# Edge sort of a ViT tower: column totals in the tower's prologue, other cuts and costs for the ranks, all row ranks beside the first experts

## The reference, cut to what matters

```python
def reference(x, ...):
    h = tower(x)                       # 4 Fourier layers on 128 images
    h = h + sigmoid_attention(layernorm(h));  h = h + top_one_experts(layernorm(h))
    h = h + l1_attention(layernorm(h));       h = h + top_two_experts(layernorm(h))
    h = h + linear_attention(layernorm(h));   h = h + image_experts(layernorm(h))
    h = h + linear_attention2(layernorm(h));  h = h + graph_experts(layernorm(h), edge_index)
    return h
# graph_experts scores its 4 experts by attention over a graph of 16384 nodes:
src = concat([edge_index[0], arange(M)]);  dst = concat([edge_index[1], arange(M)])   # 262144 edges, random
e = leaky_relu(a_src[src] + a_dst[dst]);   ee = exp(e - segment_max(e, dst)[dst])
alpha = ee / segment_sum(ee, dst)[dst];    agg = segment_sum(h[src] * alpha, dst)
```

## Time and profile before

| | us |
|---|---|
| median of 3 runs | 9904.97 (9897.18 to 9914.8) |
| the profiled execution's own time | 9901.73 |
| its span in the trace | 9899.3 |

### The profile page before, as it was taken

One profiled execution on the slowest core, in us unless ns is written; L12 is line 12 of the kernel. 1 busy time (PEld: TensorE's weight loads), 2 busy tenths in 40 slices (PEclk: granted clock), 3 DMA queues, 4 the chain that ended last, 5 costly groups with the idle time before them and its releaser, 6 DMA issues. The chain is left out here.

```text
span 9899.3 us, 199234 instructions
## 1 busy us (share of the span) xinstructions
PE 7887.8 (80%) x83028; PEld 4645.0 (47%) x83028; DVE 6833.7 (69%) x10375; ACT 4661.2 (47%) x10721; POOL 5516.5 (56%) x5545
## 2 busy tenths in 40 slices
PE   3688899989989895687888888877667688888837
PEld 2466566656656663322222222223322577777732
DVE  6799888810000587677999999985644588888852
ACT  5344444444444443235778778762333333333312
POOL 0177777777777000554666656654564377777730
PEclk7799999989999997688999999995667699999966
DMA  5000101010010000000000000000100022222210
GB/s 180 21 23 24 40 24 46 25 38 23 23 38 23 31 23 27 11 2 1 2 2 2 2 2 2 2 2 1 2 1 1 20 46 46 45 45 47 50 45 9
DMA packets 275512, 246.92 MB, mean 25 GB/s; under 512 B 204721, under 2 KB 258865, under 8 KB 268916
## 3 DMA queue, kind: packets, MB, share of 16 engines
q1 hardware_dynamic: 97300, 214.07, 6.7%
q0 software_dynamic: 177312, 20.11, 3.5%
HBM read 174.02 MB, written 59.78 MB: 24 GB/s over the span
## 5 line engine op out<-in xcount | busy, mean ns | idle before, releaser
L2558 POOL DMA_INDIRECT sorted<-by_row_rows,r_pos x2112 | 2083.0, 986 | 2167.8 <-ACT e_xt L1395 837.9
L2735 POOL DMA_INDIRECT sorted<-r_rows,r_pos x2112 | 2135.9, 1011 | 1108.5 <-issue 643.2
L2231 DVE TENSOR_TENSOR a_top<-bank,a_k 128x2048 f32<-128x2048 f32 x896 | 1972.4, 2278 | 9.7 <-ACT a_qs L2286 8.4
L3034 PE MATMUL bank<-g_parts,g_hot 128*128 128x256 bf16 x11088 | 1329.8, 287 | 246.5 <-issue 134.4
L3017 POOL DMA_INDIRECT g_g<-table,g_el x1188 | 1153.5, 971 | 362.1 <-issue 362.1
L3034 PEld LDWEIGHTS bank<-g_parts,g_hot 128*128 128x128 bf16 x11088 | 1133.5, 103 | 442.6 <-issue 142.4
L2433 PE MATMUL bank<-a_top,sc_pick_row 128*32 128x512 f32 x7168 | 953.4, 615 | 305.9 <-DVE a_top L2231 290.1
L2695 DVE TENSOR_TENSOR_SCAN r_work<-r_hit,r_base 128x528 f32<-128x528 bf16 (+7 forms) x1028 | 1073.3, 1044 | 33.6
L2279 ACT ACTIVATE a_over<-a_k,a_qs 128x64 f32<-128x64 f32 x4096 | 1021.3, 336 | 0.0
L880 DVE TENSOR_TENSOR f_qa<-f_qa,bank 128x512 f32<-128x512 f32 x128 | 82.2, 684 | 1315.8 <-PE bank L651 1113.1
L651 PEld LDWEIGHTS bank<-f_from_y,f_space 128*128 128x128 f32 x6144 | 724.1, 194 | 316.5 <-issue 160.7
(11 more groups left out here) (595 smaller groups left out, 11375.3 us busy)
## 6 DMA issues: line engine op xcount, KB each, us to landing
f_wm<-folded SPq DMA_DIRECT2D x16, 4608.0 KB
sorted<-r_rows,r_pos POOLq DMA_INDIRECT x2112
sorted<-by_row_rows,r_pos POOLq DMA_INDIRECT x2112, 2.1
g_near<-near SPq DMA_DIRECT2D x231, 128.0 KB
states<-g_st SPq DMA_DIRECT2D x33, 768.0 KB, 3.8
g_g<-table,g_el POOLq DMA_INDIRECT x1188
fp_raw<-t_modes SPq DMA_DIRECT2D x4, 2304.0 KB, 15.1
folded<-fp_turned SPq DMA_DIRECT2D x16, 576.0 KB, 11.1
```

The source lines that it names most:

```text
L2231: v.tensor_tensor(top[:, n % RD].rearrange("p q (h s) -> p q h s", s=S), q, kk, ALU.max).then_inc(top_done, 1)
L2558: p.indirect_dma_start(out=self.dst, out_offset=bass.IndirectOffsetOnAxis(ap=self.idx[:, k:k + 1], axis=0), in_=self.rows[:, k, :], in_off ...
L2735: p.indirect_dma_start(out=self.dst, out_offset=bass.IndirectOffsetOnAxis(ap=self.pos[:, at:at + 1], axis=0), in_=self.rows[:, part % 2, a ...
L3034: last = pe.matmul(out, hot[:, n % HB, k, j * P:(j + 1) * P], parts[:, k, s].rearrange("p f i -> p (f i)"), start=(k == 0 and s == 0), sto ...
```

## The change

1. In the prelude SP stores the 4 projections ahead of layer 1's folded stores instead of at the end.
2. The totals of the column counts move from slot 0 to the prologue of the first group, between L560 and L572; PE waits for the offsets (`based`) at the second step of the lift.
3. `EARLY_PAIRS` falls from 34 to 26: 8 pairs go from the prelude (15 to 7 behind layer 2) to slot 0 (4 to 12).
4. `COLUMN_CUTS` and `ROW_CUTS` change: column parts of 132, 176, 264, 484, 528, 528 become 176, 176, 264, 528, 440, 528, and row parts of 560, 560, 576, 416 become 4 x 528.
5. The planner's cost of a rank of w columns is 0.77 + 0.00343 w instead of 0.4 + 0.0042 w, and the capacity of slot 0 is 172 instead of 110. Slots 0 to 5 then hold 111, 31, 31, 31, 48, 29 items (before 102, 43, 38, 38, 54, 28). Row work starts in slot 52, not 53 (items of slots 52 to 56: 9, 17, 11, 15, 25; before from 53: 13, 17, 15, 24). `RELOAD_CHUNKS` becomes 4, 8, 16, 28.
6. The tower ranks 134 rows (122 before), so that two row parts are stored at its end. e0 ranks 8 in its norm and 86 in its units (8 and 56 before), e1 none (8 and 34 before).
7. POOL's second sends: 23 for each tile of `l1_attention` (20 before), 128 in e1 (112), none in l2 (96), 208 in e2 as before, none in l3 (112).

```diff
@@ fno_prelude, SP
                 for l in range(LAYERS):
+                    if l == 1:
+                        sp.wait_ge(proj_ready, 1)
+                        for n in range(LAYERS):
+                            sp.dma_start(f.projections[n], ...).then_inc(proj_kept, 16)
                     sp.wait_ge(fold_turned, NW * (l + 1))
...
-                sp.wait_ge(proj_ready, 1)
-                for l in range(LAYERS):
-                    sp.dma_start(f.projections[l], ...).then_inc(proj_kept, 16)
                 sp.wait_ge(proj_kept, 16 * LAYERS)
@@ fno, PE: prologue
                     pe.wait_ge(x1_moved, (gi + 1) * PAIRS)
+                    if gi == 0:
+                        totals(P, 1)
                     for pos in range(NF):
+                        if gi == 0 and pos == 1:
+                            pe.wait_ge(based, 1)
@@ fno, PE: use
-                        for m, bins, at in ((1, P, column_offset_at), (2, ROW_BINS, row_offset_at)):
-                            if n == at:
-                                ... totals ...
-                                pe.wait_ge(based, m)
+                        if n == row_offset_at:
+                            totals(ROW_BINS, 2)
+                            pe.wait_ge(based, 2)
@@ the planner
-COLUMN_CUTS = (0, 132, 308, 572, 1056, 1584, COLS)
-ROW_CUTS = (0, 560, 1120, 1696, COLS)
+COLUMN_CUTS = (0, 176, 352, 616, 1144, 1584, COLS)
+ROW_CUTS = (0, 528, 1056, 1584, COLS)
-EARLY_PAIRS = 34
+EARLY_PAIRS = 26
-RELOAD_CHUNKS = (8, 12, 20, 28)
+RELOAD_CHUNKS = (4, 8, 16, 28)
-TILE_SENDS = 20
+TILE_SENDS = 23
```

More of the change, by code:

```diff
@@ L262, in _ @@
                 for l in range(LAYERS):
+                    if l == 1:
+                        sp.wait_ge(proj_ready, 1)
+                        for n in range(LAYERS):
+                            sp.dma_start(f.projections[n], proj[:, n].rearrange("p c o y -> p (c o y)")).then_inc(proj_kept, 16)
                     sp.wait_ge(fold_turned, NW * (l + 1))
@@ L394, in fno @@
     row_done_at = [next(n for n in range(UNITS * CHUNKS) if by_rows[n + 1] >= ROW_FIRST + (part + 1) * ROW_BINS) for part in range(TOWER_PARTS)]
-    column_offset_at = next(n for n in range(UNITS * CHUNKS) if columns[n + 1] >= COLUMN_FIRST)
     row_offset_at = next(n for n in range(UNITS * CHUNKS) if by_rows[n + 1] >= ROW_FIRST)
@@ L535, in _, with totals @@
             def _(pe):
+                def totals(bins, m):
+                    pe.wait_ge(counted, m)
+                    pe.matmul(t.bank[4][:, 0:bins], t.before[:, :], ranks.hist[:, 0:bins], start=True, stop=True)
+                    pe.matmul(t.bank[5][:, 0:bins], t.ones[:, :], ranks.hist[:, 0:bins], start=True, stop=True).then_inc(summed, 1)
                 def prologue(gi):
@@ L1594, in __init__, with l2_attention @@
         self.yt = sb("yt", [D + 1, CT * P])
-def l2_attention(t, wq, wkv, g1, b1, w1, w2, g2, b2, found, by_row, first_send, sends):
+def l2_attention(t, wq, wkv, g1, b1, w1, w2, g2, b2, found):
     nc = t.nc
@@ L1629, in _ @@
                 found.ask(p, where_in, asked)
-                by_row.send_some(p, first_send, sends, sent)
-                p.wait_ge(sent, 16 * sends)
             @block.tensor
@@ L1863, in _, with l3_attention @@
                         divide(s, 1)
-def l3_attention(t, n1, wq, wkv, wo, n2, by_row, first_send, sends):
+def l3_attention(t, n1, wq, wkv, wo, n2):
     nc = t.nc
@@ L2114, in _ @@
                         divide(s, 1)
-TILE_SENDS = 20
+TILE_SENDS = 23
 FIRST_SENDS = 304
-SECOND_SENDS = 112
-FLOW_SENDS = 96
+SECOND_SENDS = 128
 THIRD_SENDS = 208
-LAST_SENDS = 112
 ACT_SLOTS = 2
@@ L2590, in slot_us, with item_us @@
     if u % LAYERS == 0:
-        return 126 if u else 110
+        return 126 if u else 172
     return 54 if u % LAYERS == LAYERS - 1 else 67
+def item_us(columns):
+    return 0.77 + 0.00343 * columns
 def spread_items(costs, offset, done, first):
@@ L2600, in spread_items @@
         while done < len(costs) and spent + costs[done] <= slot_us(n):
-            if done == offset and spent > (40 if n == 0 else 18):
+            if done == offset and n and spent > 18 or n == first and n and spent > 32:
                 break
@@ L2612, in column_plan @@
     for lo, hi in zip(COLUMN_CUTS, COLUMN_CUTS[1:]):
-        costs += [0.4 + 0.0042 * (hi - lo)] * P
+        costs += [item_us(hi - lo)] * P
     return spread_items(costs, COLUMN_PAIRS, EARLY_PAIRS, 0)
 def row_plan():
-    costs = [5.0] * ROW_PARTS + [2.5] * ROW_PAIRS + [6.0] + [0.4 + 0.0042 * (hi - lo) for lo, hi in zip(ROW_CUTS, ROW_CUTS[1:]) for _ in range(ROW_BINS)]
+    costs = [5.0] * ROW_PARTS + [2.5] * ROW_PAIRS + [6.0] + [item_us(hi - lo) for lo, hi in zip(ROW_CUTS, ROW_CUTS[1:]) for _ in range(ROW_BINS)]
     return spread_items(costs, ROW_FIRST - 1, 0, ROW_CHUNK)
@@ L2626 @@
 EARLY_ITEMS = TOWER_ROWS + TAIL_ITEMS + TOKEN_ITEMS + FIRST_LAYER_ITEMS
[L2627 removed]
+UNIT_ITEMS = ROW_PARTS * ROW_BINS - EARLY_ITEMS - NORM_ITEMS
 class EdgeRank:
```

30 lines of the change are left out of this document (9 added, 21 removed).

## The result

The changed kernel takes 9799.1 us (median of four, 9776.9 to 9815.4) against 9901.1: a ratio of 0.9892, interval 0.9876 to 0.9908. That is -102, where -48 was forecast. The profiled execution took 9812.5 (span 9810.4), one of the two longer ones. A profile of a repeat of the same kernel is shown beside it: it took 9779.3 (span 9777.2), and its four runs a median of 9777.1 at a ratio of 0.9875 (0.9860 to 0.9890).

A forecast was written before the change was run, and what follows sets the result against it. In the tower DVE, PE, then POOL's last send were taken to bound; in e0 and e1, ranks ahead of gate products. -53 + 50 - 37 - 6 - 2 = -48 from 9901.7 gave 9853.7, forecast as 9857; range 9800 to 9905.

The forecast's parts named there:

- e1's term: e1 loses its 34 unit ranks (26) and two in each norm chunk (11): -37, between -22 and -48.
- e0, +50 forecast: e0 ranks 94 instead of 64: +80.8 of DVE work, of which +50 on the path, between +15 and +81.
- The slope of 0.63: In e0, two groups of equal clock: 2.05 more of DVE work made one 1.3 longer.
- Rival 2: All of e0's added ranks are on the path: +81 instead of +50, 9888; chance 0.11.
- rival 4: e0 falls to e1's low clock, 0.60 for 0.79, and grows by 175 instead of 50: 9982, slower; chance 0.07.
- The tower, -37.5 forecast: Tower's part of the -53 for prelude and tower together: slot 53 50.5 earlier, bound by POOL's last send at 3221.
- lockstep of three sends in two ranks: Tower, POOL beside column width 440: 1.53 a send, between 1.30 (as at 528) and 2.29 (one a rank).
- rivals 1 and 3: Tower, width 440: sends pass as at 528, 9821, chance 0.15; or one send a rank, 9947, slower, chance 0.07.
- The prelude, -15.5 forecast: Eight pairs leave the prelude (19.2 of DVE), partly offset by the projections' 8.10 of SP ahead of layer 3's load.
- The bound of -19.2: Prelude's far bound: none of the projections' 8.10 of SP time delays layer 3; the other is -11.1.
- l3, 0 forecast: l3 loses its sends but gains nothing, as they end before DVE does.

The follow-up runs named there:

- again2: The changed kernel run once more, unchanged, on the chip of the third rows-from-slot-53 variant: 9799.2 us, ratio 0.9895.
- the memsets: Two runs of the changed kernel with one DVE memset, 128x1024 or 128x256, added behind each e1 unit's gate product: 9852.9 and 9830.2 us.
- the small memset: The changed kernel with one 128x256 DVE memset added behind each unit's gate product in e1: 9830.2 us, ratio 0.9925.

## Why the prediction was wrong

**The direction and the tower's mechanism held, the sum did not.** Forecast 9857, range 9800 to 9905; measured 9799.1, just below the range. By stages, the forecast's -48 stands against -89 in the profiled execution and -122 in the repeat. Three terms of the sum missed by 11 to 12 each in the same direction (the tower, e0, l3) and the prelude by 3; with e1 at -38 they still leave the profiled execution, 9812.5, inside the range. What takes the repeat's profile (9779.3) below it is e1, 37 shorter in it.

**The step that failed is e1's term,** "Units: 241.1 - 215.1 = 26", which took e3's units as e1 without ranks. e3 shows a clock of 0.63. e1 without ranks came to 273 to 285 at 0.69 to 0.74 in eight profiles and to 302 to 309 at 0.60 to 0.62 in three: -62 to -74, or -38 to -45, where the term's bounds were -22 and -48. Only the longer kind was in the forecast. From the first gate product to the last, the units took 231.3 before, 201.5 in the changed kernel's profile and 163.5 in its repeat; e3's took 201.7 before. So e3's price was that of the low clock, and that the profiled execution shows -38 for -37 is the luck of its clock. The term's other part held: the norm, up to its last move on ACT, fell from 77.6 to 66.5, by the 11 that were forecast. The changed kernel's profiled executions differ by the same stage: those at 9812.5 and 9814.6 (the change and again2) have e1 at 309, the one at 9779.3 has 273. How the old 347 divides can be read from the memsets: with 124 of DVE the stage took 314, with 167 it took 334, with the ranks (187) 347, so 0.5 to 0.6 per microsecond of DVE work at clocks of 0.57 to 0.61; carried down to the 103 that stay without ranks that is about 303, an estimate that agrees with the 302 to 309 of the low profiles. The rest, down to 273, goes with the clock.

**e0, +50 forecast, +38 measured (+29 to +39 over all runs with its 94 ranks).** The slope of 0.63 came from two groups at full clock; over the stage the 75 of added DVE time (469.0 - 393.8, forecast 80.8) cost 0.39 to 0.51 each. Rival 2 (all of it on the path) and rival 4 (the fall to e1's clock) did not come: e0 stays at 0.78 to 0.81. (The gaps of e1 that rival 4 goes by are smaller than it says: 241.1 - 191.1 = 50 in 16 groups are 3.1 of idle PE in 4 units.) But the slope isn't one number. Past 94 ranks it is above 1.4 for DVE's 18 more and 1.0 for its 40 more, both at a clock of 0.77, so the forecast's straight line was wrong in shape too. What bends it is open.

**The tower, -37.5 forecast, -49 measured.** Each step stood where it was put: slot 0 -38.2 (forecast -36.9), the offsets hidden with 2.7 to spare (forecast 3), slot 12 earlier by 104 (forecast 100), the images held behind the reload (21 instead of 35), slot 53 bound by POOL. The mis-sized term is POOL's: 1144 sends were there at 1986 (forecast 2000) and the last at 3208 (forecast 3221). Of these 13, the first send gave 4 (401 for 405), the 212 sends beside width 440 gave 5, the rest lies in small parts; the row parts were then read 1.3 behind the last send, where the forecast took 5. The rank of 440 was the forecast's 2.29, and its lockstep of three sends in two ranks, 1.53, is there in the rows above. What it left out are DVE's pauses between ranks, in which a send takes 1.26. (For the same reason the 231 sends beside width 528 in the earlier trace rows stood beside 96 ranks and not some 115.) By the Trainium skill ("SBUF — State Buffer", "Who interferes with whom") the blocked one of two such instructions waits for the whole of the other. The send of 1.75, which starts behind a running count and ends behind its end, agrees; the counts, 1.13 or 1.14 long, show no wait for a send that started ahead of them, and there the measurement decides. With 203 sends beside 116 ranks, rivals 1 and 3 both fell.

**The prelude, -15.5 forecast, -18 measured.** The pairs are all of it. The load of layer 3's raw weights was issued at 118.71 where it was at 117.35, and layer 3's transposes start 2.4 later than with the stores at the end, not the 4 that I took off; the stores that left the end make up for that. The bound of -19.2 was nearly right.

**l3, 0 forecast, -11 measured,** is one of three lengths of a stage whose clock varies. It was not in the sum. Apart from POOL's sends no engine has more work before than after; PE and its weight loads alone are busy for longer, at the lower clock. **l2** (-7 against -6), the sigmoid attention and `l1_attention` were as forecast; 23 sends a tile cost nothing.

**The range** took its low end from POOL and from e0's lower bound. e1's clock was in neither: the stage stood at 0.57, a higher clock was worth up to 37 more than the term, and the low end would have needed that.

## What to carry to other kernels

A stage whose granted clock lies between the two levels can come out at several lengths with the same work (here e1 between 273 and 309, l3 at 182, 188 or 193). Put the ends into the range, with the same group of work at either level from the trace, and don't take the price from another stage that sits at the low one. Where a chain on a slow engine (here 2112 sends) runs beside the main work, walk it to its end and ask who waits there: it made the hold at group 2 free and every microsecond of slot 0 count. And when work is moved out of one stage into another, measure the receiving stage at two amounts; its answer bends.

## What was not expected of the hardware

In e1 the full clock comes and goes by groups of four units. A group took 10.2 with PE busy 7.7 at full clock, or 15.3 at the low one. The order of the two is not noise: the profiles of the changed kernel and of again2 show the same 15 lengths from gate product to gate product to within 0.1. Over the eleven profiles without work in front of the product, the number of groups at 0.60 or less is 0 in the lengths of 273 to 275, 1 to 3 in those of 279 to 285, and 7 or 8 in those of 302 to 309. With the small memset the groups ran from 10.6 at 1.00 to 15.8 at 0.50; with 1.1 us more of PE work a group they took 13 to 18 at 0.50 to 0.78 (all but the first group in both). With more PE work the clock was lower: PE was busy 268 of 347 in that run, 184 of 273 in the repeat (and a busy microsecond at the low clock holds less work: the same group has 13.58 of it at 0.50 and 7.70 at 1.00). The Trainium skill ("TensorE: Matmul & The Clock Gate", "What's actually happening") says that activity releases a throttle that is the default; by that the added products would have helped, and here they did the opposite. e3, with almost the same instructions, had a clock between 0.58 and 0.65 over 248 of its some 270 us in each of fourteen profiles, of before, of the change and of the variants. What else tips it is open: no run here separates the length of a group from the amount of work in it. The same holds for l3's three lengths, which return to a tenth of a microsecond (182.3 in nine profiles, on several chips).
